# Expert weights and gathered token rows turned by DMA transposes instead of TensorE transposes

## What is computed

```python
gating, idx = jax.lax.top_k(affinity, k)          # k = 128 per batch and expert, 8 experts
x_in = x[bidx, idx]                               # gathered token rows, 256 features
h = silu(einsum("bekd,eid->beki", x_in, w_gate)) * einsum("bekd,eid->beki", x_in, w_up)   # i = 1024
x_e = einsum("beki,edi->bekd", h, w_down)
out = zeros_like(x).at[bidx, idx].add(gating[..., None] * x_e)
```

## Time and profile before

| | |
|---|---|
| median of 3 runs | 2128.46 us (2126.9 to 2134.37) |
| profiled execution, its own time | 2130.58 us |
| its span in the trace | 2128.7 us |
| PE busy / DVE / ACT / POOL | 1969.5 / 1228.1 / 945.7 / 583.5 us |
| expert part, first step to last down | 1039 to 2117 us |

### The profile page before, as it was taken

How to read it: one execution, slowest core, us unless ns; L and a number is a source line. 1 busy time by engine, 2 the same in 40 slices (tenths; PEclk the granted TensorE clock), 3 DMA queues, 4 the chain that set the end, 5 groups by cost and what they waited for, 6 DMA issues and landing times.

```text
span 2128.7 us, 43898 instructions
## 1 busy us (share of the span) xinstructions
PE 1969.5 (93%) x14952; PEld 1197.8 (56%) x14952; DVE 1228.1 (58%) x2953; ACT 945.7 (44%) x1792; POOL 583.5 (27%) x492
## 2 busy tenths in 40 slices
PE   3899999999999999996599999999999999999997
PEld 2455555555555555554256566565656666565665
DVE  4777877887778778776653434434343434435332
ACT  2355555555555555664243333333333333434332
POOL 2112222222222222214223232323323232332312
PEclk9899999999999999997699999999999999999999
DMA  3533444444444444334122231322222232311212
GB/s 109 116 114 112 132 134 117 120 121 129 136 139 132 130 139 116 114 91 149 51 69 50 50 60 40 73 52 55 50 52 52 69 60 41 60 27 34 41 15 26
DMA packets 141572, 179.73 MB, mean 84 GB/s; under 512 B 23544, under 2 KB 123008, under 8 KB 141440
## 3 DMA queue, kind: packets, MB, share of 16 engines
q1 hardware_dynamic: 116864, 144.39, 23.3%
q0 software_dynamic: 24576, 33.57, 10.0%
HBM read 118.63 MB, written 58.72 MB: 83 GB/s over the span
## 4 chain that ended last, share of the span: by engine, by line
PE 48%; DVE 2%; DMA 1%; issue 1%; POOL 0%; ACT 0%; DVEq 0%; ACTq 0%; POOLq 0%
PE bank L1002 10%; PE bank L1003 10%; PE bank L1004 10%; PE bank L1019 5%; PE bank L1018 5%; PE bank L1017 5%; PE bank L972 2%; PE bank L986 1%; DMA out<-y,row_now 1%; DVE top_at L1078 1%; DVE work L1081 1%; DVE top L1076 1%; DVE h L1125 0%; ACT h L1055 0%; POOL out L936 0%
## 5 line engine op out<-in xcount | busy, mean ns | idle before, releaser
L534 ACT ACTIVATE prob<-bank 128x512 f32<-128x512 f32 x640 | 372.0, 596 | 235.8 <-PE bank L423 228.3
L936 POOL DMA_INDIRECT out<-y,row_now x128 | 201.6, 1575 | 703.8 <-ACT y L1063 679.4
L1125 DVE TENSOR_TENSOR h<-bank,silu 128x512 f32<-128x512 f32 x256 | 176.8, 691 | 342.6 <-PE bank L1004 281.3
L403 PE MATMUL bank<-ks,qs 96*128 96x128 bf16 (+3 forms) x1024 | 281.1, 307 | 64.1 <-DVE mx L622 41.0
L1055 ACT ACTIVATE h<-h 128x512 bf16<-128x512 f32 x256 | 161.1, 629 | 391.3 <-DVE h L1125 391.3
L622 DVE CUSTOM_DVE_ANT_0 masked<-bank,causal 128x384 f32<-128x384 f32 (+1 forms) x512 | 304.3, 616 | 45.5 <-PE bank L403 43.9
L1128 DVE TENSOR_TENSOR h<-h 128x512 bf16<-128x512 f32 x256 | 177.3, 693 | 179.3 <-ACT h L1055 179.3
L1017 PE MATMUL bank<-downT,h 128*128 128x256 bf16 x1024 | 279.2, 273 | 0.0
L1019 PE MATMUL bank<-downT,h 128*128 128x256 bf16 x1024 | 279.2, 273 | 0.0
L1018 PE MATMUL bank<-downT,h 128*128 128x256 bf16 x1024 | 279.2, 273 | 0.0
L421 PE MATMUL bank<-qs,ks 98*128 98x512 bf16 (+3 forms) x1024 | 268.8, 302 | 0.1
(11 more groups left out here) (156 smaller groups left out, 3086.2 us busy)
## 6 DMA issues: line engine op xcount, KB each, us to landing
qs<-q_parts SPq DMA_DIRECT2D x384, 64.0 KB, 2.6
ks<-k_parts SPq DMA_DIRECT2D x384, 64.0 KB, 2.7
q_parts<-q_sb SPq DMA_DIRECT2D x32, 384.0 KB, 3.1
k_parts<-k_sb SPq DMA_DIRECT2D x32, 384.0 KB, 3.2
x_t<-in_x SPq DMA_DIRECT2D x16, 512.0 KB, 4.1
ctx_t<-in_ctx SPq DMA_DIRECT2D x16, 512.0 KB, 4.9
res_t<-in_x SPq DMA_DIRECT2D x16, 512.0 KB, 5.5
out<-x SPq DMA_DIRECT2D x16, 512.0 KB, 3.1
```

The source lines that it names most:

```text
L403: last = nc.tensor.matmul(dst[:, h * w:(h + 1) * w], qs[0:STACK, gr, h0 + h, i * P:(i + 1) * P], ks[0:STACK, gr, h0 + h, 0:w], start=True, ...
L534: nc.scalar.activation(prob[:, gr % 2, h0:h0 + nh, POFF[tiles[0]]:POFF[tiles[0]] + w], sc_bank[SC_BANK[k]][:, 0:nh * w].rearrange("p (h w) ...
L936: nc.gpsimd.indirect_dma_start(out_rows, bass.IndirectOffsetOnAxis(ap=row_now[:, par, CHUNK * c + s:CHUNK * c + s + 1], axis=0), y[:, c % ...
```

## The change

The split into high and low now comes first, in the layout in which the weights were loaded (`w_nat`), and SP turns the split bf16 tiles with DMA transposes: two of 128x2048 (512 KB each, one high, one low) for each of gate, up and down, and one of 128x512 (128 KB) for each `tok` job. PE, and DVE for the tokens, have no part in it any more. `weights` jobs on ACT and DVE keep their places in the order. The transposes are issued by SP: those of `tok` at the job's place, those of gate, up and down at that of their last job (k = 3, 7, 11).

```diff
+    w_nat = {n: sb(ctx, f"{n}_nat", [P, 2, IT * D], BF16) for n in w_raw}
+    w_in = {n: sb(ctx, f"{n}T", [P, 2, 2, IT, NH2, P], BF16) for n in ("gate", "up")}
+    w_out = sb(ctx, "downT", [P, 2, 2, NH2, IT, P], BF16)
...
         def _(sp):
+                if p[0] == "tok":
+                    wait_apart(sp, S["up_filled"], (e * CHUNKS + c - 1) * IT, passed["sp"])
+                    wait_apart(sp, gathered[c % 2][s], (e * 2 + c // 2 + 1) * 16, passed["sp"])
+                    dst = tokT[:, c % 2, :, :, s * P:(s + 1) * P].rearrange("p r d t -> p (r d) t")
+                    sp.dma_start_transpose(dst, rows[:, c % 2, s, :]).then_inc(tok_ready[c % 2], 16)
+                elif p[0] == "load":
-                    wait(sp, S["w_turned"], (e - 1) * WJOBS + 4 * (PARTS.index(n) + 1))
+                    wait(sp, S["w_lo"], (e - 1) * WJOBS + 4 * (PARTS.index(n) + 1))
...
+                elif p[0] == "weights" and p[4] % 4 == 3:
+                    if n == "down":
+                        wait_apart(sp, S["down_done"], (e - 1) * CHUNKS * CHUNK, passed["sp"])
+                    else:
+                        wait_apart(sp, S["up_filled"], (e - 1) * CHUNKS * IT, passed["sp"])
+                    wait_apart(sp, S["w_lo"], e * WJOBS + k + 1, passed["sp"])
+                    for r in range(2):
...
+                        sp.dma_start_transpose(dst, w_nat[n][:, r, :]).then_inc(w_ready[n], 16)
...
         def _(pool):
-                        wait_apart(pool, S["tok_turned"], (n - 1) * CHUNK, passed["pool"])
+                        wait_apart(pool, tok_ready[c % 2], (e * 2 + c // 2) * 64, passed["pool"])
...
         def _(pe):
-                        last = nc.tensor.transpose(weights_bank(e, k)[:, j * P:(j + 1) * P], src, ident[:, :])
-                    last.then_inc(S["w_turned"], 1)
...
-                        last = nc.tensor.transpose(to[:, j * P:(j + 1) * P], rows[:, c % 2, s, j * P:(j + 1) * P],
-                                                   identb[:, :])
...
-                        wait(pe, S["tok_read"], (n + 1) * CHUNK)
-                        wait(pe, S["w_lo"], (e + 1) * WJOBS)
+                        wait(pe, tok_ready[c % 2], (e * 2 + c // 2 + 1) * 64)
+                        wait(pe, w_ready["gate"], (e + 1) * 32)
+                        wait(pe, w_ready["up"], (e + 1) * 32)
...
+                        wait(pe, w_ready["down"], (e + 1) * 32)
...
         def _(act):
+                    wait(act, raw_loaded[part], (e + 1) * 16)
+                    wait(act, w_ready[part], e * 32)
+                    nc.scalar.activation(weights_nat(0, k), weights_raw(k), ACT.Copy).then_inc(S["w_hi"], 1)
...
         def _(dve):
+                    nc.vector.tensor_tensor(weights_nat(1, k), weights_raw(k), weights_nat(0, k), ALU.subtract)\
+                        .then_inc(S["w_lo"], 1)
...
-                    nc.vector.tensor_copy(dst, tok_bank[:, :].bitcast(BF16)[:, 0:4 * P].rearrange(
-                        "p (j t) -> p j t", j=4)).then_inc(S["tok_read"], 1)
```

More of the change, by code:

```diff
@@ L794, in experts @@
     out_rows = g["out"].rearrange("b t d -> (b t) d")
-    gate_bank, up_bank, y_bank, tok_bank, w_bank = bank[0:2], bank[2:4], bank[4:6], bank[6], bank[7]
+    gate_bank, up_bank, y_bank = bank[0:2], bank[2:4], bank[4:6]
     CHUNK = BATCH // 4
@@ L816, in experts @@
              "down": sb(ctx, "down_raw", [P, NH2, INNER], F32)}
-    w_in = {n: sb(ctx, f"{n}T", [P, 2, 2, NH2, INNER], BF16) for n in ("gate", "up")}
-    w_out = sb(ctx, "downT", [P, 2, 2, IT, D], BF16)
+    w_nat = {n: sb(ctx, f"{n}_nat", [P, 2, IT * D], BF16) for n in w_raw}
+    w_in = {n: sb(ctx, f"{n}T", [P, 2, 2, IT, NH2, P], BF16) for n in ("gate", "up")}
+    w_out = sb(ctx, "downT", [P, 2, 2, NH2, IT, P], BF16)
     rows = sb(ctx, "rows", [P, 2, CHUNK, 2 * D], BF16)
@@ L827, in experts @@
     names = ("rows_turned", "rows_copied", "top_found", "top_located", "top_taken", "at_float", "top_turned",
-             "base_made", "row_made", "gating_made", "row_now_made", "gate_now_made", "w_turned", "w_copied", "w_hi", "w_lo",
-             "tok_turned", "tok_read", "gate_filled", "up_filled", "silu_done", "h_done", "h_hi", "h_lo",
+             "base_made", "row_made", "gating_made", "row_now_made", "gate_now_made", "w_hi", "w_lo",
+             "gate_filled", "up_filled", "silu_done", "h_done", "h_hi", "h_lo",
              "down_done", "y_read")
@@ L832, in experts @@
     raw_loaded = {n: sem(f"{n}_raw_loaded") for n in w_raw}
+    w_ready = {n: sem(f"{n}_ready") for n in w_raw}
+    tok_ready = [sem(f"tok_ready{i}") for i in range(2)]
     gathered = [[sem(f"gathered{i}{j}") for j in range(CHUNK)] for i in range(2)]
@@ L882, in is_first, with weights_raw, weights_nat @@
         return isinstance(e, int) and e == 0
-    def weights_bank(e, k):
-        return tok_bank if is_first(e) and k % 2 else w_bank
-    def weights_dst(par, r, k):
+    def weights_raw(k):
         part, q = PARTS[k // 4], k % 4
-        if part == "down":
-            return w_out[:, par, r, 2 * q:2 * q + 2, :].rearrange("p i d -> p (i d)")
-        return w_in[part][:, par, r, q // 2, (q % 2) * 512:(q % 2 + 1) * 512]
+        flat = w_raw[part][:, :, :].rearrange("p a b -> p (a b)")
+        return flat[:, q * 512:(q + 1) * 512]
+    def weights_nat(r, k):
+        part, q = PARTS[k // 4], k % 4
+        return w_nat[part][:, r, q * 512:(q + 1) * 512]
     with nc.Block() as block:
@@ L898, in piece @@
             def piece(p):
-                if p[0] == "load":
+                if p[0] == "tok":
+                    _, e, _, c, s = p
+                    wait_apart(sp, S["up_filled"], (e * CHUNKS + c - 1) * IT, passed["sp"])
[3 more added lines that the diff above has]
+                elif p[0] == "load":
                     _, e, _, _, n = p
-                    wait(sp, S["w_turned"], (e - 1) * WJOBS + 4 * (PARTS.index(n) + 1))
+                    wait(sp, S["w_lo"], (e - 1) * WJOBS + 4 * (PARTS.index(n) + 1))
                     sp.dma_start(w_raw[n][:, :, :], src[n][e].rearrange("(o p) i -> p o i", p=P))\
                         .then_inc(raw_loaded[n], 16)
+                elif p[0] == "weights" and p[4] % 4 == 3:
+                    _, e, par, _, k = p
+                    n = PARTS[k // 4]
+                    if n == "down":
[4 more added lines that the diff above has]
+                    for r in range(2):
+                        if n == "down":
+                            dst = w_out[:, par, r, :, :, :].rearrange("p d i c -> p (d i) c")
+                        else:
+                            dst = w_in[n][:, par, r, :, :, :].rearrange("p i d c -> p (i d) c")
+                        sp.dma_start_transpose(dst, w_nat[n][:, r, :]).then_inc(w_ready[n], 16)
             run(sp, piece, BEFORE, AFTER)
@@ L917, in piece @@
                     k = p[4]
-                    wait(pool, S["w_copied"], k + 1)
                     wait(pool, S["w_hi"], k + 1)
-                    nc.gpsimd.tensor_tensor(out=weights_dst(par, 1, k), in0=h32[:, k % 2, :],
-                                            in1=weights_dst(par, 0, k), op=ALU.subtract).then_inc(S["w_lo"], 1)
+                    nc.gpsimd.tensor_tensor(out=weights_nat(1, k), in0=weights_raw(k), in1=weights_nat(0, k),
+                                            op=ALU.subtract).then_inc(S["w_lo"], 1)
                 elif kind == "gather":
@@ L955, in piece @@
                 n = e * CHUNKS + c
[L956 to L971, removed]
-                        last = nc.tensor.transpose(weights_bank(e, k)[:, j * P:(j + 1) * P], src, ident[:, :])
-                    last.then_inc(S["w_turned"], 1)
-                elif kind == "columns" and is_first(e):
+                if kind == "columns" and is_first(e):
                     pe.wait_ge(S["at_float"], 1)
@@ L979, in piece @@
                     nc.tensor.transpose(gate_bank[1][:, P:2 * P], top[:, :], ident[:, :]).then_inc(S["top_turned"], 1)
[L980 to L985, removed]
-                        last = nc.tensor.transpose(to[:, j * P:(j + 1) * P], rows[:, c % 2, s, j * P:(j + 1) * P],
-                                                   identb[:, :])
-                    last.then_inc(S["tok_turned"], 1)
                 elif kind == "up":
@@ L999, in piece @@
                         for dh in range(NH2):
-                            hi, lo = (w_in[name][:, par, r, dh, it * P:(it + 1) * P] for r in range(2))
+                            hi, lo = (w_in[name][:, par, r, it, dh, :] for r in range(2))
                             xh, xl = (tokT[:, c % 2, r, dh, :] for r in range(2))
@@ L1009, in piece @@
                         wait(pe, S["h_lo"], (n + 1) * IT)
+                        wait(pe, w_ready["down"], (e + 1) * 32)
                     if s % 2 == 0:
                         wait(pe, S["y_read"], (n - 1) * CHUNK + s + 2)
-                    to = y_bank[s // 2][:, (s % 2) * D:(s % 2 + 1) * D]
```

(11 more changed lines are left out.)

## The result

The changed kernel takes 2070.85 us (median of 4, 2069.55 to 2071.93) against 2129.95 before (2126.9 to 2134.37): ratio 0.972, 95% interval 0.970 to 0.974. The forecast was 2069.

The account below looks back on a forecast made before the run. PE was taken to bound the expert part (busy 1067 of 1078 us). 2130.6 - 64.4 + 4.0 + 1.5 = 2071.7, and the median stands 2.1 below the profiled execution: 2069 us, range 2060 to 2240.

Parts of the forecast that it names:

- The PE time removed: After the first step: 124 tok jobs at 0.226 us and 84 weights jobs at 0.433 us leave PE, 64.4 us.
- The columns wait: At chunk 1 in six copies, PE arrives 0.66 us earlier and waits that much longer: 4.0 us not gained.
- The start: Before the first step, 1.12 us becomes one 128 KB DMA transpose's landing, taken as 2.6 us: 1.5 us added.
- Nothing for ACT's and DVE's new operands: In weights jobs, ACT's cast and DVE's subtraction now read SBUF, costed at nothing; 0.1 us a job would be 8.
- rival B: DVE or the wait at `columns` takes over, as transposes share DMA engines with gathers and scatters: 2080 to 2110; chance 0.06.
- 5.5 us to give back: Time returned out of the gain: 4.0 us at the `columns` wait plus 1.5 us at the first step.
- The unknown d: Time the DMA engines need for one 512 KB transpose, taken as 2 to 4 us; a tok transpose takes d/4.
- free bounds of 4.8, 6.3 and 7.6: Largest d, in us, at which transposes stay hidden before the next chunk, in chunks 3, 2 and 1.
- The room in chunk 3: From the weights job's low part to the next chunk: 12.7 us for 2.25d plus 2 us of landing.
- D: Rival: SP's transpose queue comes late, each 256-byte piece costing 68 ns, d = 8.7: 2235 us (2150 to 2300); chance 0.17.
- E: Rival: DMA bound, pieces at 139 ns, d = 17.8, an expert taking 190 us against 134: about 2620 us; chance 0.10.
- The break-even: At d = 7.3 us, stalls at chunk starts reach the 8.1 us an expert gains; from there the change loses.

Follow-up runs that it names:

- the halves: Two runs against the kernel before: only token rows turned by DMA, 2108.5 us (ratio 0.990); only weights turned by DMA, 2097.7 us (0.985).
- eighth kernel: The changed kernel with every DMA transpose replaced by a plain DMA of the same tile, leaving weights and token rows unturned: 2071.1 us (ratio 0.972).

## Why the prediction was right

**The PE time removed** (64.4 us) was right: the chunks came out at 31.20 us as worked out, and the halves' chunks at their own sums.

**The columns wait** was right in direction but mis-sized: 4.0 us forecast, 0.2 measured. PE's wait for the multiply did rise, from 6.1 to 9.4 us. But the forecast took this wait for the whole cost. In the kernel before the same wait of DVE also held back its token copies, for which PE waited another 2.0 us, and 2.1 more were lost that the view shows as no wait. With the token jobs gone 1.0 of such loss is left, so the excess of the six chunks moved only from 10.2 to 10.4 us. The halves show it apart: with the weights jobs alone removed it rose by 2.9 us, close to the 2.6 of this reasoning; with the token jobs alone removed it fell by 0.9, where the reasoning has a rise of 1.4.

**The start** was mis-sized: 2.2 us (12.2 - 10.0) and not 1.5. The forecast took 2.6 us, the landing of a plain 64 KB DMA; from the issue of the fourth transpose to the first step it is 3.1. The eighth kernel shows that a plain DMA of 128 KB is no quicker here.

**Nothing for ACT's and DVE's new operands** held. DVE's subtraction stayed at 684 to 688 ns (the trace's 0.68 before), and PE has no wait for either in the expert part. So nothing of rival B showed: a chunk with three weights jobs in it is as long, 31.20 us, as one in the last expert, which has none.

From the start of the first step to the last down: 1077.3 us before (1039.22 to 2116.48) and 1015.5 after (1041.69 to 2057.15). The 61.8 are 64.4 - 0.2 - 2.4, and the 2.4 are at the turn of the loop on the engines, which no step of the forecast foresaw:

```profile
1572.68 0.39 PE L1002 MATMUL bank<-tokT,gateT 128*128 128x512 bf16 x1 [2.31 <-issue]
```

```profile
1540.93 0.60 PE L1001 MATMUL bank<-tokT,gateT 128*128 128x512 bf16 x1 [3.40 <-issue]
```

PE's wait there, whose releaser the profile doesn't show, is 3.40 us after the change against 2.31, and behind it the clock is at its lower level, so that the next chunk, to 1573.49, takes 32.56 us and not 31.20. The wait differs from run to run of the experiments too (2.3 to 4.4 us), and why is open.

**Luck in the last microseconds.** The forecast had 5.5 us to give back, 4.0 + 1.5. The trace has 5.1 in other places: 0.2 at `columns`, 2.4 at the loop's turn, and 2.5 by which the first step comes later. That 2069 met 2070.85 so closely is two errors that cancel. That some 64 us go and little comes back is the mechanism.

**The unknown d**, read as the time in SP's queue, was 2.3 to 2.9 us, in the range taken (2 to 4), so the free bounds of 4.8, 6.3 and 7.6 were not reached. The room in chunk 3, forecast as 12.7 us, is 12.6 (1783.37 to 1795.99). A token transpose, though, takes 1.2 us of the queue, not d/4 = 0.6: a quarter of the bytes is half of the time. The rivals D and E fell on the price of a 256-byte piece. The packets added to q1 are 286336 - 116864 = 169472, of 248 bytes in the mean (186.35 - 144.39 MB), and q1's time rose from 0.233 x 16 x 2128.7 to 0.361 x 16 x 2069.4 us, by 4017: 24 ns each, a third of D's 68.

**The break-even** of d = 7.3 was too hopeful. With three times the big transposes the six took 18.2, 15.3 and 14.4 us in chunks 3, 2 and 1, so d near 9.1, 7.6 and 7.2 by the forecast's measure. Its formulas then give stalls of 9.8, 3.2 and 0 us; the trace has 9.9, 3.6 and 0.9. So the stalls were right, and yet the kernel was 83 us slower than before. Two prices were missing: the lower clock behind a wait, some 28 us in all or 4 an expert, half of the 8.1 that an expert gains; and the start, where PE waits 24 us longer than in the changed kernel. The transposes themselves were also slower at some places: those of `down` into the spare tiles took 3.45 us each in chunk 3, where POOL's scatters run, and 3.3 at the start, ahead of the first scatter, against 2.5 for those of gate and up at the start. That POOL's DMAs cause this was not tried.

## What to carry to other kernels

Where PE bounds and the DMA engines are a quarter busy, transposes moved to DMA are paid back in full PE time: count them by the distance between starts (0.433 us for four f32 blocks, 0.226 for four bf16). Then look at what stands behind them in the issuing queue: the small transfer that the next stage waits for must be issued ahead of the large ones that nothing waits for yet. That order was worth 117 us where the queue was long and nothing where it was short. And count a wait by the distance between chunk starts, not by the waits that a view lists: `columns` cost 10 us in both kernels where the lists had 8.1 and 9.4, and one piece moved by four steps brought them back in either.

## What was not expected of the hardware

At the start, back to back, 512 KB transposes between tiles of the on-chip memory leave SP's queue every 2.4 us, some 215 GB/s, where a plain copy of the same tile is issued in 0.56 us and lands in 3.3 to 3.8 instead of 4.8 to 5.0 (changed kernel above, eighth below):

```profile
1006.60 5.12 SPq L930 DMA_TRANSPOSE upT<-up_nat  x2
1011.77 4.85 SPq L930 DMA_TRANSPOSE downT<-down_nat  x2
```

```profile
1006.06 1.11 SPq L931 DMA_DIRECT2D upT<-up_nat  x2
1010.51 1.11 SPq L931 DMA_DIRECT2D downT<-down_nat  x2
```

So a transposing DMA took 1.3 to 1.5 times as long to its landing and over four times as long in the issuing queue. The Trainium skill (Advanced Engine Details and Errata, X-Bar Transpose (TRN2)) calls them as fast as regular ones; these rows say less than that. The 1309 ns that the Trainium skill (VectorE: DVE Perf Modes, The three transpose paths) gives for one 128x128 block do not add up over blocks: a tile of 16 took 2.4 us of the queue.
